# Layer 0's router: split operands with eight stationary columns, and a turn behind the up products

## What is computed

```python
def _L0_ffn_ref(x, W_up, W_down, W_gate, W_expert):
    logits = jnp.einsum('bsd,ed->bse', x, W_gate)
    routing_weights, selected_experts = jax.lax.top_k(logits, TOP_K)
    shared_out = jnp.einsum('bsd,od->bso', jax.nn.relu(jnp.einsum('bsd,od->bso', x, W_up)), W_down)
    rw = jax.nn.softmax(routing_weights, axis=-1)
    expert_out = jnp.einsum('bsd,do->bso', x, W_expert)
    moe_out = jnp.sum(rw, axis=-1, keepdims=True) * expert_out
    return shared_out + moe_out
...
x = x + jnp.tanh(g_ffn[0]) * _L0_ffn_ref(_layernorm(x, axis=-1), L0_ffn_W_up, L0_ffn_W_down, L0_ffn_W_gate, L0_ffn_W_expert)
```

## Time and profile before

| | |
|---|---|
| runs | 3624.12, 3630.9, 3637.68 us |
| profiled execution, its own time | 3627.06 us |
| its span, first to last instruction | 3625.2 us |
| busy: TensorE, VectorE, ScalarE, GpSimd | 89%, 72%, 50%, 39% of the span |
| mean granted TensorE clock | 0.943 |
| data moved by DMA | 478.69 MB, mean 132 GB/s |

### The profile page before, as it was taken

How to read it: one execution, slowest core, us unless ns; L and a number is a source line. 1 busy time by engine, 2 the same in 40 slices (tenths; PEclk the granted TensorE clock), 3 DMA queues, 4 the chain that set the end, 5 groups by cost and what they waited for, 6 DMA issues and landing times. The chain is left out here.

```text
span 3625.2 us, 43497 instructions
## 1 busy us (share of the span) xinstructions
PE 3213.1 (89%) x14628; PEld 1934.1 (53%) x14628; DVE 2598.1 (72%) x3488; ACT 1804.9 (50%) x3413; POOL 1402.6 (39%) x956
## 2 busy tenths in 40 slices
PE   7869898999996888799999999999999887997995
PEld 3347644333333555455555555555555456785763
DVE  7853678877765888377777877777777754665786
ACT  5544333666662445355655555555655332664220
POOL 1121179000000000166666667666666644223540
PEclk9878999999998999899999999999999988998998
DMA  3136636222218200254445444444454356665321
GB/s 128 48 119 243 246 118 157 56 59 61 56 29 177 29 1 1 90 168 152 165 154 168 158 165 161 154 153 166 152 168 137 105 194 197 241 249 190 140 70 58
DMA packets 229750, 478.69 MB, mean 132 GB/s; under 512 B 36239, under 2 KB 69647, under 8 KB 213664
## 3 DMA queue, kind: packets, MB, share of 16 engines
q1 hardware_dynamic: 223296, 459.19, 39.6%
q0 software_dynamic: 6240, 16.81, 1.3%
HBM read 387.51 MB, written 92.06 MB: 132 GB/s over the span
## 5 line engine op out<-in xcount | busy, mean ns | idle before, releaser
L2346 POOL TENSOR_TENSOR l2x_inflow<-l2x_dtu,l2x_rows_b 128x512 f32<-128x512 f32 x256 | 431.5, 1686 | 330.9 <-DVE l2x_state L2235 308.7
L178 POOL TENSOR_TENSOR ln_work<-ln_work,minus_half 128x4 f32<-128x4 f32 (+1 forms) x34 | 33.2, 976 | 1044.9 <-DVE ln_work L166 1044.8
L2235 DVE TENSOR_TENSOR_SCAN l2x_state<-l2x_decay,l2x_inflow 128x512 f32<-128x512 f32 x256 | 381.7, 1491 | 17.2 <-ACT l2x_decay L2109 17.2
L1305 DVE TENSOR_REDUCE l1x_mx<-psum 128x2 f32<-128x1024 f32 x256 | 308.3, 1219 | 96.0 <-PE psum L1147 94.5
L2362 POOL TENSOR_TENSOR l2x_y_sum<-l2x_y_sum,l2x_state 128x512 f32<-128x512 f32 x224 | 342.1, 1527 | 33.0 <-DVE l2x_state L2244 33.0
L2049 ACT ACTIVATE l2x_probs<-psum,l2x_soft,l2x_norms 128x512 f32<-128x512 f32 x256 | 195.5, 775 | 319.4 <-DVE l2x_soft L2173 319.4
L1262 ACT ACTIVATE l1x_split<-psum 128x1024 f32<-128x1024 f32 x256 | 262.0, 1024 | 154.8 <-PE psum L1147 154.8
L126 PE MATMUL psum<-l2x_probs_t,l2x_v_tok 128*128 128x512 f32 x512 | 240.5, 614 | 31.5 <-ACT l2x_probs_t L212 25.9
L2244 DVE TENSOR_TENSOR l2x_state<-l2x_state,l2x_rows_c 128x512 f32<-128x512 f32 x256 | 252.6, 987 | 6.7 <-issue 0.3
L126 PE MATMUL psum<-l2x_xt,l2x_wq 128*128 128x512 f32 x512 | 231.0, 595 | 7.7 <-issue 6.3
L126 PE MATMUL psum<-l2x_kt,l2x_qt 128*128 128x512 f32 x512 | 230.5, 593 | 4.0 <-ACT l2x_probs L2049 4.0
(11 more groups left out here) (446 smaller groups left out, 7359.5 us busy)
## 6 DMA issues: line engine op xcount, KB each, us to landing
l2x_rows_b<-l3x_xd_dram SPq DMA_DIRECT2D x256, 256.0 KB, 3.6
l2x_rows_c<-l3x_xd_dram SPq DMA_DIRECT2D x256, 256.0 KB, 3.5
l2w_raw<-l_w SPq DMA_DIRECT2D x38, 1024.0 KB, 6.2
l2x_wkv<-l2x_kv_dram SPq DMA_DIRECT2D x32, 1024.0 KB, 7.0
l2w_raw<-l_w SPq DMA_DIRECT2D x38, 512.0 KB, 4.6
l1x_heads_dram<-l1x_stage SPq DMA_DIRECT2D x32, 512.0 KB, 3.3
l2x_wq<-l_wq SPq DMA_DIRECT2D x16, 1024.0 KB, 7.1
l2x_wo<-l_wo SPq DMA_DIRECT2D x16, 1024.0 KB, 5.4
```

What stands on the lines that cost most here:

```text
L1305: main.drain(dve.tensor_reduce(mx[:, gg % 2, :, j, t], g["psum"][:, b:b + 2, :], AX.X, ALU.max), f"m{n}_0", banks=2)
L2235: dve.tensor_tensor_scan(state[:, s % KEPT, :], decay[:, s % 3, :], inflow[:, s % 3, :], 0.0, ALU.mult, ALU.add).then_inc(scan_done, 1)
L2346: pool.tensor_tensor(inflow[:, s % 3, :], dtu[:], rows_b[:, s % 3, :], ALU.mult).then_inc(inflow_ready, 1)
```

## The change

The router's product is turned round. The router weights are split once into `router_parts` (ScalarE hi, VectorE lo), and `split_product` makes one product group of 12 with the router's 8 columns stationary and the 512 tokens of `xt_parts` moving, into 8 partitions of bank `logits`. VectorE copies these to an SBUF tile `logits` (128 partitions, the rest zero from one memset at the start). Behind the up products four float32 transposes of 128x128 turn it into bank `router`, each token tile at a distance of 128 columns, and VectorE takes its maxima from there. VectorE's steps move with it: the copy stands behind the first part of `rounded`, and the maxima and the difference behind the four `l0f_ht_lo`. ScalarE no longer writes `l0f_xt`, and that tile is gone. The ring keeps 18 jobs: `logits` comes in, the spare goes, and `router` moves behind `h3`. ScalarE waits for the weights (`weights_in`) ahead of its loop instead of ahead of `weight_round(2)`.

```diff
@@ -683,7 +683,8 @@
         up, down, expert = split_weights = [[sb(f"{n}_{part}", [P, DC, D], F32R) for part in ("hi", "lo")]
                                             for n in ("up", "down", "expert")]
         router = sb("router", [P, DC, 8])
-        xt = sb("xt", [P, DC, S])
+        router_parts = [sb(f"router_{part}", [P, DC, 8], F32R) for part in ("hi", "lo")]
+        logits = sb("logits", [P, S])
         xt_parts, ht = [[sb(f"{n}_{part}", [P, DC, S], F32R) for part in ("hi", "lo")] for n in ("xt", "ht")]
         top = sb("top", [P, ST, 8])
         small = sb("small", [P, 8, ST])
@@ -693,9 +694,11 @@
         sums, all_sums, total = sb("sums", [P, 12]), sb("all_sums", [P, P, 12]), sb("total", [P, 3])
         sums_dram = nc.dram_tensor("l0f_sums_dram", [P, 12], F32).ap()
         w_abs = g["w_abs"]
-        ring = Ring(sem, "l0f", range(6), [(f"xt{c}", "dve") for c in range(DC)] + [("router", "dve")]
-                    + [(f"h{m}", "dve") for m in range(DC)]
-                    + [(f"{k}{t}", "dve") for t in range(ST) for k in ("sh", "ex")] + [("spare", None)])
+        ring = Ring(sem, "l0f", range(6), [(f"xt{c}", "dve") for c in range(DC)] + [("logits", "dve")]
+                    + [(f"h{m}", "dve") for m in range(DC)] + [("router", "dve")]
+                    + [(f"{k}{t}", "dve") for t in range(ST) for k in ("sh", "ex")])
+        cleared = sem("cleared")
+        router_hi, router_lo, logits_done = sem("router_hi"), sem("router_lo"), sem("logits_done")
         weights_in, top_ready, exp_ready, dve_steps, w_hi, w_lo, x_hi, h_hi = [sem(n) for n in (
             "weights_in", "top_ready", "exp_ready", "dve_steps", "w_hi", "w_lo", "x_hi", "h_hi")]
         (t_done, t_rounded, t_scaled, t_steps, sums_out, sums_in, total_ready, scale_ready) = [sem(n) for n in (
@@ -769,16 +772,21 @@
             pe.wait_ge(weights_in, 32)
             with pe.Fori(0, NB) as i:
                 xt_fill(pe, g, ln, ring, i)
-                ring.wait_for(pe, i, free="router", drained=["xt2", "xt3"])
-                for t in range(ST):
-                    last = product(pe, bank("router")[:, t * 8:t * 8 + 8],
-                                   [(xt[:, c, t * P:(t + 1) * P], router[:, c, :]) for c in range(DC)])
-                ring.fill(last)
+                pe.wait_ge(router_lo, 1)
+                ring.wait_for(pe, i, free="logits", drained=["xt2", "xt3"])
+                ring.fill(split_product(pe, bank("logits")[0:8, :], [
+                    ([r[:, c, :] for r in router_parts], [x[:, c, :] for x in xt_parts]) for c in range(DC)]))
                 pe.wait_ge(w_lo, 1)
                 for m in range(DC):
                     ring.wait_for(pe, i, free=f"h{m}")
                     ring.fill(split_product(pe, bank(f"h{m}"), [([w[:, c, m * P:(m + 1) * P] for w in up],
                                                                  [x[:, c, :] for x in xt_parts]) for c in range(DC)]))
+                pe.wait_ge(logits_done, i + 1)
+                ring.wait_for(pe, i, free="router")
+                for t in range(ST):
+                    last = pe.transpose(bank("router")[:, t * P:(t + 1) * P], logits[:, t * P:(t + 1) * P],
+                                        g["ident"][:])
+                ring.fill(last)
                 pe.wait_ge(w_lo, 3)
                 for t in range(ST):
                     for job, act_t, w in ((f"sh{t}", ht, down), (f"ex{t}", xt_parts, expert)):
@@ -793,6 +801,8 @@
 
             act.wait_ge(early["up_in"], 16)
             weight_round(0)
+            act.wait_ge(weights_in, 32)
+            act.activation(router_parts[0][:], router[:], ACT.Copy).then_inc(router_hi, 1)
 
             def absolute(m):
                 act.wait_ge(t_in[m % 2], (m // 2 + 1) * 16)
@@ -824,12 +834,10 @@
             for i in range(NB):
                 for c in range(DC):
                     ring.wait_filled(act, i, f"xt{c}")
-                    act.activation(xt[:, c, :], bank(f"xt{c}"), ACT.Copy).then_inc(x_hi, 1)
                     act.activation(xt_parts[0][:, c, :], bank(f"xt{c}"), ACT.Copy).then_inc(x_hi, 1)
                 if i == 0:
                     act.wait_ge(early["down_in"], 16)
                     weight_round(1)
-                    act.wait_ge(weights_in, 32)
                     weight_round(2)
                 if i == 2:
                     totals()
@@ -861,17 +869,32 @@
                     dve.wait_ge(t_scaled, m - 11)
                     dve.tensor_scalar(tile, tile, -1.0, ROUND, ALU.max, ALU.add).then_inc(t_rounded, 1)
 
+            dve.memset(logits[:], 0.0).then_inc(cleared, 1)
+            dve.wait_ge(cleared, 1)
+            dve.wait_ge(router_hi, 1)
+            dve.tensor_tensor(router_parts[1][:], router[:], router_parts[0][:].bitcast(F32), ALU.subtract
+                              ).then_inc(router_lo, 1)
             for i in range(NB):
                 st.begin(i)
                 for c in range(DC):
-                    dve.wait_ge(x_hi, (i * DC + c + 1) * 2)
+                    dve.wait_ge(x_hi, i * DC + c + 1)
                     ring.drain(dve.tensor_tensor(xt_parts[1][:, c, :], bank(f"xt{c}"), xt_parts[0][:, c, :].bitcast(F32),
                                                  ALU.subtract), f"xt{c}")
                 rounded(i, 0)
+                ring.wait_filled(dve, i, "logits")
+                if i:
+                    ring.wait_filled(dve, i - 1, "router")
+                ring.drain(dve.tensor_copy(logits[0:8, :], bank("logits")[0:8, :]), "logits")
+                ring.wait_for(dve, i, drained=["logits"])
+                dve.sem_inc(logits_done, 1)
+                for m in range(DC):
+                    dve.wait_ge(h_hi, i * DC + m + 1)
+                    ring.drain(dve.scalar_tensor_tensor(ht[1][:, m, :], bank(f"h{m}"), 0.0, ht[0][:, m, :].bitcast(F32),
+                                                        ALU.max, ALU.subtract), f"h{m}")
                 ring.wait_filled(dve, i, "router")
                 st.inc(dve.memset(small[:, 7, :], 0.0))
                 for t in range(ST):
-                    ins = dve.max(top[:, t, :], bank("router")[:, t * 8:t * 8 + 8])
+                    ins = dve.max(top[:, t, :], bank("router")[:, t * P:t * P + 8])
                     if t == ST - 1:
                         ring.drain(ins, "router")
                     else:
@@ -880,10 +903,6 @@
                 ring.wait_for(dve, i, drained=["router"])
 
                 dve.tensor_tensor(small[:, 0, :], top[:, :, 1], top[:, :, 0], ALU.subtract).then_inc(top_ready, 1)
-                for m in range(DC):
-                    dve.wait_ge(h_hi, i * DC + m + 1)
-                    ring.drain(dve.scalar_tensor_tensor(ht[1][:, m, :], bank(f"h{m}"), 0.0, ht[0][:, m, :].bitcast(F32),
-                                                        ALU.max, ALU.subtract), f"h{m}")
                 rounded(i, 1)
                 dve.wait_ge(ring.drained_sem["dve"], (i + 1) * ring.who.count("dve"))
                 ln.vector(dve, i, (i + 1) % NB, lambda: ring.wait_filled(dve, i, "xt3"))
```

## The result

| | before | after |
|---|---|---|
| median of the runs | 3626.51 us (6 runs, 3620.48 to 3637.68) | 3604.53 us (6 runs, 3600.88 to 3615.34) |
| ratio to before, 95% interval | | 0.9941 [0.9928, 0.9955] |
| profiled execution: its time, span | 3627.06, 3625.2 us | 3603.29, 3601.6 us |
| mean granted clock | 0.943 | 0.949 |
| the phase, first transpose to the next phase's first | 209.39 us | 184.15 us |

The change makes the kernel faster by 0.59%, 22 us. The forecast was 3604.0 in a range of 3596 to 3618. The phase can be read closer than the runs: from its first transpose to the first of the next phase, the forecast was -27.0 and the trace has -25.2.

A forecast was written before the change was run, and what follows sets the result against it. TensorE was taken to set the length of layer 0's feed-forward. Terms 5.3 + 13.4 + 9.6 - 1.3 = 27.0 us, taken from the 3630.9 us median, gave 3604 us, range 3596 to 3618.

The forecast's parts named there:

- Term 1: TensorE's wait for l0f_xt_lo ahead of the router shrinks without ScalarE's l0f_xt copies, saving 5.3 us over four bodies.
- Term 2: Layer 0 feed-forward router: 32 records a body, 24.5 us in all, become 12 products a body, 11.1 us; 13.4 saved.
- The twin in layer 2: Existing layer-2 products with nine columns and the same split; twelve take 2.78 us at full clock, used to size the new products.
- If the clock never falls: Condition for the 48 up products per body running at full clock throughout, giving back 9.6 us.
- Term 3: Up products of four bodies run at full clock, 44.5 us in place of 54.1, saving 9.6 us.
- The reading from layer 2: Nine-column products alone run at clock 0.50, then 0.95 follows; so products using 8 of 128 columns will hold the clock.
- 1.95 is nearest to 1.84, so I take kept: The remaining 1.95 us gap ahead of the logits products resembles a 1.84 us layer-2 gap where the clock stayed 1.00.
- Term 4: Added transposes hide behind the up products; later maxima lengthen residual waits in bodies 2 and 3, losing 1.3 us.
- Rival 1: Clock still falls in each body: 7.2 to 20.7 us lost, time 3611 to 3624.6, middle 3618; chance 0.13.
- rule on transposes: Trainium skill's rule that transposes don't count as busy like other products, so transposes plus gap would make one idle stretch.
- Rival 2: In bodies 2 and 3 the gain returns as longer residual wait; 14 us stay, 3617 us; chance 0.12.
- Rival 3: Late weight loads in bodies 2 and 3, about 9 us left from issue to rounding; slower, up to 3650; chance 0.04.

The follow-up runs named there:

- e1_keep_copy: Changed kernel with ScalarE's unread float32 copies of the chunks put back, VectorE waiting for both copies; 3613.52 us, ratio to before 0.9967.
- e2_old_router_one_copy: Kernel before without the float32 copies, its old router products taking only the tokens' hi part; 3614.60 us, ratio to before 0.9965.
- e4_first_residual_early: Changed kernel with the first token tile's two residual adds and their small factors moved ahead of VectorE's layer norm; 3594.75 us, ratio to before 0.9918.
- e8_old_router_filled: e2_old_router_one_copy with 14 transposes into an unused PSUM bank ahead of the router products; 3607.22 us in one run.
- e9_fill_alone: Changed kernel with only 14 transposes into an unused PSUM bank added ahead of the logits products; 3598.25 us, ratio to before 0.9938.
- e6_last_split_first: e4_first_residual_early with ScalarE splitting the last part of the last body between its two ternary passes; 3601.21 us, ratio to before 0.9928.

## Why the prediction was right

- **Term 1**, 5.3 us: 5.8. The waits are 1.90 us three times (forecast 1.95, though its own 3.53 - 1.55 is 1.98) and 1.41 in body 0 (1.6). `e1_keep_copy` gives the same 5.8 back.
- **Term 2**, 13.4: 11.9. 24.5 less 2.76 + 2.78 + 4.31 + 2.78 = 12.6. The twin in layer 2 gave the right 2.78; the step that failed is the clause "If the clock never falls", which the sum took as given. It fell once, under body 2's logits products, at a cost of 1.5 us.
- **Term 3**, 9.6: 9.4 by the cuts of the tables, and 8.8 from the first up product to the first down product (59.7 us in the four bodies before, 51.0 after); the tables cut the up products at the first transpose now, some 0.16 us ahead of their end. The size was near; of the two grounds, one did the work. The text hung it first on the gap and second on the form of the products. `e1_keep_copy` has the gap of before and keeps the up products at 11.2; `e2_old_router_one_copy` has the gap of after and does not. The reading from layer 2, that the split products with few stationary columns raise the clock and so hold it, was the part that counted: it was an inference from one rise, and the up products of all four bodies and the logits products of three bear it out. "1.95 is nearest to 1.84, so I take kept" was too firm: at 1.9 us it falls in one body of three, and in 4 of 12 over all kernels.
- **Term 4**, -1.3: -1.2. The residual waits are 3.82 and 3.79 where 3.8 was forecast, and the transposes, sixteen in all, are hidden.
- **Sum**: 5.8 + 11.9 + 8.8 - 1.2 = 25.3 of terms, 25.2 in the phase. With term 3 as the tables cut it the sum is 25.9.
- **Rival 1** is the one that holds in part: one stretch in one body, 1.5 us, near its cheap end of 1.8 and not in each body. By the rule on transposes that the forecast weighed, the clock would have fallen in all four; it falls in one, and the filled waits speak against the rule.
- **Rival 2** does not hold for body 2: it is 6.2 us shorter (55.15 to 48.94), with no growth of the residual wait beyond term 4. In body 3 (55.63 to 50.49) it comes nearer than the forecast knew. The next phase's first load is issued 5.38 us behind the issue of the last split store (418.74 to 424.12), and so it was before (443.90 to 449.27, 5.37), as in `e4_first_residual_early` (5.36), where TensorE is done 8 us ahead. So this store very likely ends the phase in all three. The change gains in body 3 because the store moves with the up products; the next gain there, in `e4_first_residual_early`, is lost to it.
- **Rival 3** does not hold. In body 2 the second piece is asked for at 338.33 and its rounding begins at 348.83, 10.5 us later, where "about 9 us are left" was said. VectorE never waits for it; its one wait at a rounding, 2.6 us, is for the scale from GpSimd, and it was 2.9 before.
- **The total**: the forecast took 27 us from 3630.9. With more runs before's median is 3626.51, and the gain between the medians is 22.0 us. So 3604.0 against 3604.53 is in part luck: a gain put 5 us too high met a starting point 4.4 too high. The gain of the phase, 25.2 for 27.0, is the fair measure of the working.

## What to carry over

When a clock is low under a block of large products, look at the form of what stands ahead of it: products with short moving sides cost time behind them too (some 9 us here, under products that nobody changed). A wait ahead of a dense stretch can be filled with idle transposes into a free bank: that gave 4.7 us at waits of 3.5 us, and 0.6 in one profile at 1.9, which the runs cannot tell from nothing. And before two waits late in a phase are removed, read what ends the phase: here a store that TensorE's table of waits does not show.

## What the runs showed of the hardware that was not expected

- 32 float32 records with 8 moving columns, back to back, with TensorE 100% busy (3.60 us at 1.00), are followed by a stretch at the low clock under full-size products (`e8_old_router_filled`, bodies 1 and 2; in body 3 it begins within the records), where 12 products of 8 stationary columns and 512 moving are not (all bodies of `e9_fill_alone`).
- Float32 transposes in a wait keep the clock up: 28 of them, with at most 0.48 us of wait left behind them, and no fall in four bodies, against four falls behind 3.5 us (2.3 in body 0). They don't raise it each time: behind body 0's 16 transposes the clock rose by 246 us in the kernels before and after, and in `e2_old_router_one_copy`, with the same transposes, it was 0.50 up to the up products.
- The rest of the kernel, the same work in each of these programs, took 3166.3 to 3184.0 us in ten profiled executions and 3206.5 in one. Most of the difference lies in the phase that follows, and it is the clock. The stretch from 460 to 1060 us, in the kernel after and then in `e6_last_split_first`, from their tables of stretches:

```profile
460.00:1060.00 600.00, 560.60 (x3845) 238.84 (x3844) 472.11 (x585) 341.97 (x413) 127.24 (x126) 0.99 0.30 75
```

```profile
460.00:1060.00 600.00, 565.98 (x3692) 235.31 (x3690) 463.60 (x569) 328.43 (x393) 119.60 (x117) 0.93 0.30 73
```

In the same 600 us TensorE has 3692 records in place of 3845, at 0.93 in place of 0.99. What sets off these stretches at half clock, in work that none of the edits touches, was not tried and stays open. It is why phases are compared here and not single times: a change of 5 us is smaller than this spread.
